# Selecting four features per row once for six products of a feature crossing, with grouped products and roundings

## The chip, the core and the metric

One NeuronCore of a Trainium2 chip runs the whole program. The metric is the device time of one execution in microseconds; lower is better. TensorE (PE) multiplies matrices into PSUM, VectorE (DVE) and ScalarE (ACT) do elementwise work and copies, GpSimd (POOL) starts the gathers from the embedding tables, SyncE (SP) starts the other transfers.

## What is computed

A recommender's forward pass for 512 samples with 39 categorical features. Each feature of a sample is looked up as a vector of 16 numbers; e has the shape 512 x 39 x 16. Two layers of a feature crossing follow, then a small dense tower:

```python
# _cin(e, [W0, W1]); m, n run over features, d over the 16 numbers
z  = einsum('bmd,bnd->bdmn', e, e)          # all 39 x 39 products per number
X1 = einsum('bdp,po->bod', z, W0)           # 1521 x 128
z  = einsum('bmd,bnd->bdmn', e, X1)
X2 = einsum('bdp,po->bod', z, W1)           # 39*128 x 128
h  = concat([sum_d(X1), sum_d(X2), dense_ctx])   # 512 x 272
h  = relu(h @ W_top1 + b1); h = relu(h @ W_top2 + b2); y = h @ W_top3
```

Everything is in float32, and the kernel keeps that precision on fast matmuls by splitting operands: a number is rounded to the fast format (high part), the remainder is kept (low part), and three products (high x high, high x low, low x high) stand for one.

## The kernel before

The batch is four tiles of 128 samples. A tile is cut into four chunks of 32 samples, and a chunk's 32 x 16 = 512 columns are the moving operand. So there are 16 chunks.

The first layer needs only the products of unordered pairs of features: 39 x 40 / 2 = 780. They are laid out as 7 groups of rows (PT = 7): six of 128 pairs, and the last one with the 12 pairs left over, each three times (REST_AT), for the three products of the split. A *step* s is one such group; 7 steps make a chunk, 28 a tile (SPT), and 112 (STEPS) the batch. The features of a tile, turned to have features on the partitions, are in `xs` as three bf16 parts. In a step, PE picks one factor of each pair with a 0/1 matrix (`select`, L904) into one of two PSUM banks (`b_bank`); the other factor, `xa`, is the same for all steps, since row p of every group has feature p % 39 as its first factor. It is copied out of PSUM once per chunk (`fill_a`, `take_a`, L882, L423). DVE multiplies (`multiply`, L716) into `z`, ACT rounds to `z_hi` (`round_z`, L529), DVE takes the remainder `z_lo` two steps later (`rest_z`, L730), and PE sums with the weights `w0_hi`, `w0_lo` five steps later (LAG; `layer1`, L919 to L927). In tile 0 two of the seven groups (DIRECT) skip the split: PE multiplies them in whole float32. `z_hi` and `z_lo` have seven slots (RING), one for each step in flight, so a step overwrites the slot of seven steps before, which PE has used two steps ago. `z` has four.

After the seven groups of a chunk ACT copies `xi` (L545), PE turns it (L934), ACT and DVE split it (L551, L737), and four times per chunk PE forms a block of g (L949 to L951) in the single bank `g_bank`, which ACT copies out (`take_g`, L537) before the next block may start. The x side for this is made by `turn_a` (L891), `take_xt`, `rest_xt` and transfers into `diag`. Layer 2 (L964) uses g a tile later, 39 matmuls for a tile, spread over 26 steps (12 for tile 2).

There is no scheduler: each engine runs one loop over s with the offsets written out, and executes its instructions strictly in the order of that loop, waiting on semaphores. The offsets within a chunk (steps modulo 7): `turn_a` at 1; `fill_a` of the next chunk at 4; g blocks at 3, 5, 0, 2; copy of xi at 4, its turn at 6. The order on ACT within a step is rounding, split copies, `take_g`, `take_xi`, `round_xit`, `take_xt`, `take_a`, `take_x`. The order on PE is selection, `turn_a`, `turn_x`, `turn_xi`, g block, layer 2, `fill_a`, layer 1.

The features come in two ways: small tables by one-hot products in the first 35 us, the others by 98 indirect DMAs which GpSimd starts one after another, with a filler memset between two of them. A tile's features are split into three bf16 parts in three pieces (`SPLIT_AT`: steps of the tile before; `keep_top` and `keep_next` on ACT, L475 and L481; `rest_hi` and `rest_mid` on DVE, L634 and L641), then turned on PE in two halves (`X_AT`, L860), each copied by ACT (`take_x`, L414), and then the first `xa` chunk of the tile is filled (`A_AT`).

## Time and profile before

| | |
|---|---|
| median of 3 runs | 263.35 us (263.24 to 263.35) |
| profiled execution | 262.94 us |
| its span, first to last instruction | 260.9 us |
| mean granted TensorE clock | 0.961 |
| busy: PE, DVE, ACT, POOL | 235.9, 196.1, 168.6, 128.8 us |

Busy time is the time with an instruction running on the engine. In a list of groups, `out<-in` names the tensors, then come shapes and counts, busy time, mean duration in ns, and the idle time right before such instructions with what ended it. In a timeline the first two numbers are start and duration in us; a square bracket gives idle time before the instruction and what released it. Durations of neighbours on one engine can overlap. The granted clock is the share of full speed (2.4 GHz) which TensorE was given.

### The profile page before, as it was taken

The page shows a single profiled execution, that of the slowest core. Times are in us where ns is not written, and L with a number is a line of the kernel's source. Part 1 is how long each engine was busy: PE and PEld are TensorE (multiplying, and loading weights), DVE is VectorE, ACT ScalarE, POOL GpSimd, SP SyncE. Part 2 cuts the span into 40 slices and gives each one's busy share as a digit, 9 for nine tenths or more (in the row PEclk, how much of TensorE's full clock was granted, in tenths as well). Part 3 has the DMA queues.
Part 4 walks back from the last instruction along what each step waited for, and adds up shares of the span by engine and source line. Part 5 has one row for each costly group of instructions (what it writes and reads, how often), then busy time and mean ns, then how long its engine had stood idle before and what let it go on. Part 6 is the DMA issues. An engine that isn't in the chain of part 4 may idle for free.

```text
span 260.9 us, 5243 instructions
## 1 busy us (share of the span) xinstructions
PE 235.9 (90%) x1848; PEld 182.4 (70%) x1848; DVE 196.1 (75%) x341; ACT 168.6 (65%) x324; POOL 128.8 (49%) x180
## 2 busy tenths in 40 slices
PE   4998856989799978939999999999999999999996
PEld 4997733555466754737777777777787888898795
DVE  1799969998879999556889999879989877624001
ACT  4997555675787886547759878686757655466203
POOL 4788888888888888878888882000000000000000
PEclk9999755899999999988999999999999999999999
DMA  5920001545026540200221111010110101010000
GB/s 160 233 45 10 9 5 13 112 83 129 8 27 147 122 96 7 28 8 9 45 33 20 24 11 28 5 25 7 21 16 12 25 1 25 4 25 0 3 0 0
DMA packets 30883, 10.30 MB, mean 39 GB/s; under 512 B 21018, under 2 KB 30138, under 8 KB 30858
## 3 DMA queue, kind: packets, MB, share of 16 engines
q1 hardware_dynamic: 27722, 9.17, 16.3%
q0 software_dynamic: 3136, 0.81, 3.5%
q8 instruction: 14, 0.23, 0.4%
q14 instruction: 11, 0.09, 0.1%
HBM read 7.34 MB, written 0.00 MB: 28 GB/s over the span
## 4 chain that ended last, share of the span: by engine, by line
PE 48%; POOL 26%; DVE 12%; issue 9%; ACT 3%; DMA 2%; DVEq 0%; ACTq 0%
POOL feat L355 21%; PE s_bank L964 11%; POOL pad L353 5%; PE b_bank L904 4%; PE l_bank L925 4%; PE l_bank L927 4%; PE l_bank L926 4%; DVE z L716 3%; DVE w_sb L660 3%; DVE z_lo L730 3%; PE g_bank L949 2%; PE g_bank L950 2%; PE g_bank L951 2%; PE xi_bank L934 1%; ACT g L448 1%
## 5 line engine op out<-in xcount | busy, mean ns | idle before, releaser
L355 POOL DMA_INDIRECT feat<-tbl,ids_sb x98 | 107.3, 1095 | 29.4 <-POOL pad L353 21.1
L716 DVE TENSOR_TENSOR z<-xa,b_bank 128x512 f32<-128x512 f32 (+1 forms) x112 | 76.1, 684 | 17.3 <-PE b_bank L904 13.8
L529 ACT ACTIVATE z_hi<-z 128x512 fp32r<-128x512 f32 (+1 forms) x104 | 65.6, 630 | 18.9 <-DVE z L716 17.5
L730 DVE TENSOR_TENSOR z_lo<-z,z_hi 128x512 fp32r<-128x512 f32 x88 | 60.3, 686 | 0.0
L904 PE MATMUL b_bank<-xs,sel 117*128 117x512 bf16 (+1 forms) x112 | 45.2, 406 | 8.7 <-DVE z L716 8.6
L964 PE MATMUL s_bank<-g,w_sb 128*128 128x128 f32 x312 | 46.3, 278 | 0.0
L964 PEld LDWEIGHTS s_bank<-g,w_sb 128*128 128x128 f32 x312 | 42.2, 192 | 1.3 <-issue 0.7
L925 PE MATMUL l_bank<-z_hi,w_hi 128*128 128x512 f32 x88 | 41.8, 474 | 0.0
L904 PEld LDWEIGHTS b_bank<-xs,sel 117*128 117x128 bf16 (+1 forms) x112 | 11.5, 103 | 38.3 <-DVE z L716 20.7
L537 ACT ACTIVATE g<-g_bank 128x320 f32<-128x320 f32 x64 | 27.7, 432 | 16.3 <-PE g_bank L951 16.0
L927 PE MATMUL l_bank<-z_hi,w_lo 128*128 128x512 f32 x88 | 35.1, 399 | 0.0
L926 PE MATMUL l_bank<-z_lo,w_hi 128*128 128x512 f32 x88 | 35.0, 398 | 0.0
L949 PE MATMUL g_bank<-diag,xit_hi 128*128 128x320 f32 x64 | 29.5, 462 | 3.2 <-ACT g L537 3.2
L353 POOL MEMSET pad<- 128x192 f32 x78 | 21.3, 273 | 0.1
L950 PE MATMUL g_bank<-diag,xit_hi 128*128 128x320 f32 x64 | 20.1, 313 | 0.0
L951 PE MATMUL g_bank<-diag,xit_lo 128*128 128x320 f32 x64 | 19.9, 310 | 0.0
L927 PEld LDWEIGHTS l_bank<-z_hi,w_lo 128*128 128x128 f32 x88 | 16.8, 191 | 3.8
L949 PEld LDWEIGHTS g_bank<-diag,xit_hi 128*128 128x128 f32 x64 | 12.6, 197 | 8.1 <-issue 5.9
L925 PEld LDWEIGHTS l_bank<-z_hi,w_hi 128*128 128x128 f32 x88 | 17.1, 194 | 1.3 <-issue 0.8
L926 PEld LDWEIGHTS l_bank<-z_lo,w_hi 128*128 128x128 f32 x88 | 17.1, 194 | 0.2
L545 ACT ACTIVATE xi<-l_bank 128x512 f32<-128x512 f32 x16 | 9.6, 597 | 9.0 <-PE l_bank L922 9.0
L560 ACT ACTIVATE g<-b_bank,bt_sb 128x384 f32<-128x384 f32 (+1 forms) x8 | 3.7, 473 | 15.8 <-PE b_bank L1005 11.0
(190 smaller groups left out, 368.2 us busy)
## 6 DMA issues: line engine op xcount, KB each, us to landing
diag<-xt SPq DMA_DIRECT2D x128, 20.0 KB
w_sb<-w SPq DMA_DIRECT2D x3, 832.0 KB
feat<-tbl,ids_sb POOLq DMA_INDIRECT x98, 2.4
wt_sb<-wt SPq DMA_DIRECT2D x2, 512.0 KB, 4.7
g<-small SPq DMA_DIRECT2D x1, 770.0 KB
g<-small SPq DMA_DIRECT2D x1, 448.0 KB
w0p<-w_pair SPq DMA_DIRECT2D x1, 448.0 KB
w0m<-w_mirror SPq DMA_DIRECT2D x1, 448.0 KB
```

The costliest lines, as they stand in the source:

```text
L353: nc.gpsimd.memset(pad[:], 0.0).then_inc(rested, 1)
L355: nc.gpsimd.indirect_dma_start(feat[:, bt % 2, n * D:(n + 1) * D], None, tables[order[n]], bass.IndirectOffsetOnAxis(ids_sb[:, bt, order[n ...
L529: nc.scalar.activation(z_hi[0:rows, s % RING, :], z[0:rows, at, :], ACT.Copy).then_inc(rounded, 1)
L537: nc.scalar.activation(g[:, bt % 2, :, block * SB:(block + 1) * SB], g_bank[:, 0:SB * GW].rearrange("p (b m) -> p m b", m=GW), ACT.Copy).t ...
L716: nc.vector.tensor_tensor(target, xa[0:rows, bt % 2, c * CB:(c + 1) * CB, :].rearrange("p b d -> p (b d)"), b_bank[s % B_RING][0:rows, :], ...
L730: nc.vector.tensor_sub(low[first:rows, s % RING, :], z[first:rows, SPLITS[s] % Z_RING, :], z_hi[first:rows, s % RING, :].bitcast(f32)).the ...
L904: nc.tensor.matmul(b_bank[s % B_RING][0:ROWS[t], :], sel[:, t, 0:ROWS[t]], columns(bt, c), start=True, stop=True).then_inc(selected, 1)
L925: nc.tensor.matmul(bank[:], w0_hi[:, t, :], z_hi[:, slot, :], start=t == 0, stop=False)
L926: nc.tensor.matmul(bank[:], w0_hi[:, t, :], z_lo[:, slot, :], start=False, stop=False)
L927: nc.tensor.matmul(bank[:], w0_lo[:, t, :], z_hi[:, slot, :], start=False, stop=False).then_inc(l1_used, 1)
L949: nc.tensor.matmul(o, y_hi, x_hi, start=True, stop=False)
L964: last = nc.tensor.matmul(s2_bank[:, 0:P], w1_sb[:, order[m], :], g[:, bt % 2, m, :], start=m == 0, stop=m == F - 1)
```

## The change

1. **Rows.** The pairs are laid out anew. Each row has four features (from the 130 lines of a block design on 40 points, of which one is no feature), and a row's six products of two of the four are the six full groups. All 741 mixed pairs and the 39 squares are covered, with the last ones in the rest group, now on all 128 rows.
2. **Selections.** Per chunk one x copy (`fill_a`) and four selections (before: one and seven). The first two are copied to SBUF by ACT (`take_factor`, new; DVE takes one of them in chunk 0), the other two are read from PSUM. The products are f0f1, f0f2; then f0 times the rest factor; then f3 times f0, f1, f2; then f1f2. `turn_a` reads factor 0.
3. **Groups.** Multiplication, rounding and remainder come as four instructions per chunk (of 2, 1, 3 and 1 groups of rows) in steps 0, 2, 3 and 6 of the chunk; the remainders in steps 2, 4, 6 and 8. The rest group is third instead of last. The slots of `z_hi` and `z_lo` are fixed by the group, so a rounding waits until PE has used all its slots for the chunk before.
4. **Whole products.** One per chunk of tile 0 instead of two.
5. **Offsets.** The splits of tiles 2 and 3 move from steps 8, 14, 19 and 9, 16, 21 of the tile before to 9, 16, 23; their turns from 21, 22 and 23, 24 to 25, 26; the x copy from 24 and 26 to 27. The first chunk of these tiles has its selections in its own steps 0, 0, 1, 2 instead of ahead of it.
6. **Small ones.** `w0_rest` is made by two multiplications with 0/1 columns instead of three copies, ahead of DVE's copy of the first features.

The diff, cut to its core:

```diff
-PT = -(-PAIRS // P)
-REST = PAIRS - (PT - 1) * P
-REST_AT = (0, F, 2 * F)
-REST_LO = 64
-REST_ROWS = 96
-ROWS = [P] * (PT - 1) + [REST_ROWS]
-assert REST <= F and REST_AT[1] >= 32 and REST_AT[1] + REST <= REST_LO <= REST_AT[2] and REST_AT[2] + REST <= REST_ROWS
+PT = 7
+FACTORS = 4
+PRODUCTS = ((0, 1), (0, 2), (3, 0), (3, 1), (3, 2), (1, 2))
+REST_T = PT - 1
+REST_LO = slice(64, 98)
+T_OF = (0, 1, REST_T, 2, 3, 4, 5)
+GROUPS = ((0, 2, 0, 0), (2, 1, REST_T, 2), (3, 3, 2, 3), (6, 1, 5, 2))
+GROUP_AT = {first: k for k, (first, count, slot, at) in enumerate(GROUPS)}
+REST_AT_STEP = {2: 0, 4: 1, 6: 2, 8: 3}
+GROUP_OF = [next(k for k, g in enumerate(GROUPS) if g[0] <= u < g[0] + g[1]) for u in range(PT)]
+NG = len(GROUPS)
+SELECTS = 4
...
-DIRECT = [[1, 4], [], [], []]
+DIRECT_CHUNKS = 4
 WHOLE = 2
-Z_LAG = 2
-Z_RING = Z_LAG + 2
-LEAD = 1
+Z_SLOTS = 6
...
-SPLIT_AT = [[], [8, 14, 19], [8, 14, 19], [9, 16, 21]]
-X_AT = [[], [21, 22], [21, 22], [23, 24]]
-A_AT = [0, 24, 24, 26]
+SPLIT_AT = [[], [8, 14, 19], [9, 16, 23], [9, 16, 23]]
+X_AT = [[], [21, 22], [25, 26], [25, 26]]
+A_AT = [0, 24, 27, 27]
+SELECT_AT = [-4, -2, -1, 0]
+TILE_SELECT_AT = [None, [-4, -2, -1, 0], [0, 0, 1, 2], [0, 0, 1, 2]]
...
             def take_a(i):
-                bt, c = divmod(i, CPT)
                 act.wait_ge(*after(turn_filled, "a", i, 0))
                 k = fill["a", i, 0][0]
-                nc.scalar.activation(xa[:, bt % 2, c * CB:(c + 1) * CB, :],
-                                     turn_banks[k][:].rearrange("p (b d) -> p b d", d=D),
-                                     ACT.Copy).then_inc(turn_taken[k], 1)
+                if i >= 2:
+                    act.wait_ge(product, NG * (i - 1))
+                nc.scalar.activation(factors[:, i % 2, 0, :], turn_banks[k][:], ACT.Copy).then_inc(turn_taken[k], 1)
+
+            def take_factor(i, k):
+
+                act.wait_ge(selected, SELECTS * i + k + 1)
+                if i >= 2:
+                    act.wait_ge(product, NG * (i - 1))
+                nc.scalar.activation(factors[:, i % 2, 1 + k, :], b_bank[k][:], ACT.Copy).then_inc(factor_taken, 1)
...
-            def round_z(s):
-                rows = ROWS[s % PT]
-                if direct(s):
+            def round_z(i, k):
+                if direct(i, k):
                     return
-                at = SPLITS[s] % Z_RING
-                act.wait_ge(product, s + 1)
-                if s >= RING:
-                    act.wait_ge(l1_used, s - RING + 1)
-                nc.scalar.activation(z_hi[0:rows, s % RING, :], z[0:rows, at, :], ACT.Copy).then_inc(rounded, 1)
+                first, count, slot, at = GROUPS[k]
+                act.wait_ge(product, NG * i + k + 1)
+                if i:
+                    act.wait_ge(l1_used, (i - 1) * PT + first + count)
+                nc.scalar.activation(z_hi[:, slot:slot + count, :], z[:, at:at + count, :],
+                                     ACT.Copy).then_inc(rounded, 1)
...
+                for i, q in SELECT_STEPS.get(s, []):
+                    if q < 2 and i:
+                        take_factor(i, q)
+                if s < STEPS and s % PT in GROUP_AT:
+                    round_z(s // PT, GROUP_AT[s % PT])
...
+            def z_free(i, k):
+
+                if (i, k) in SPLITS:
+                    dve.wait_ge(remainder, SPLITS[i, k] + 1)
+
+            def multiply(i, k):
...
+                if k == 0:
+                    for q in range(2):
+                        dve.wait_ge(*taken_factor(i, q))
+                    dve.wait_ge(*after(turn_taken, "a", i, 0))
+                    z_free(i - 1, 0)
+                    target = z[:, 0:2, :]
+                    one = factors[:, i % 2, 0, :].unsqueeze(1).broadcast_to([P, 2, CH])
+                    other = factors[:, i % 2, 1:3, :]
+                elif k == 1:
+                    dve.wait_ge(selected, SELECTS * i + 3)
+                    z_free(i - 1, 1)
+                    z_free(i - 1, 3)
+                    target, one, other = z[:, 2, :], factors[:, i % 2, 0, :], b_bank[0][:]
+                elif k == 2:
+                    dve.wait_ge(selected, SELECTS * i + 4)
+                    z_free(i - 1, 2)
+                    target = z[:, 3:6, :]
+                    one = factors[:, i % 2, :, :]
+                    other = b_bank[1][:].unsqueeze(1).broadcast_to([P, 3, CH])
                 else:
+                    if direct(i, k):
+                        if i == 0:
+                            dve.wait_ge(zeroed, 4)
+                        if i >= WHOLE:
+                            dve.wait_ge(l1_used, (i - WHOLE + 1) * PT)
+                        target = whole[i % WHOLE][:]
+                    else:
+                        z_free(i, 1)
+                        target = z[:, 2, :]
+                    one, other = factors[:, i % 2, 1, :], factors[:, i % 2, 2, :]
+                nc.vector.tensor_tensor(target, one, other, ALU.mult).then_inc(product, 1)
...
+            def rest_z(i, k):
+                if direct(i, k):
                     return
+                first, count, slot, at = GROUPS[k]
+                dve.wait_ge(rounded, SPLITS[i, k] + 1)
+                if i:
+                    dve.wait_ge(l1_used, (i - 1) * PT + first + count)
+                if k == 1:
+                    nc.vector.tensor_sub(z_hi[REST_LO, slot, :], z[REST_LO, at, :],
+                                         z_hi[REST_LO, slot, :].bitcast(f32)).then_inc(remainder, 1)
+                else:
+                    nc.vector.tensor_sub(z_lo[:, slot:slot + count, :], z[:, at:at + count, :],
+                                         z_hi[:, slot:slot + count, :].bitcast(f32)).then_inc(remainder, 1)
...
-            def select(s):
-
-                i, t = divmod(s, PT)
-                bt, c = divmod(i, CPT)
-                if s >= B_RING:
-                    pe.wait_ge(product, s - B_RING + 1)
-                if t == 0:
+            def select(i, q):
+
+                if q == 0:
                     features_there(i)
-                nc.tensor.matmul(b_bank[s % B_RING][0:ROWS[t], :], sel[:, t, 0:ROWS[t]], columns(bt, c),
+                if q < 2:
+                    if i:
+                        pe.wait_ge(product, NG * (i - 1) + 2 + q)
+                else:
+                    pe.wait_ge(*taken_factor(i, q - 2))
+                nc.tensor.matmul(b_bank[q % B_RING][:], sel[:, q, :], columns(*divmod(i, CPT)),
                                  start=True, stop=True).then_inc(selected, 1)
...
+                for i, q in SELECT_STEPS.get(s, []):
+                    select(i, q)
```

## Rows read from the trace of the kernel before

**Rows 1.** The page: the span, and each engine's busy time and share.

```profile
span 260.9 us, 5243 instructions
...
PE 235.9 (90%) x1848; PEld 182.4 (70%) x1848; DVE 196.1 (75%) x341; ACT 168.6 (65%) x324; POOL 128.8 (49%) x180
```

**Rows 2.** Busy us by stretch: PE, weight loads, DVE, ACT, POOL, granted clock, DMA.

```profile
66.00:108.00 42.00, 37.32 (x197) 25.59 (x198) 39.11 (x69) 32.17 (x67) 35.10 (x51) 1.00 0.32 66
115.00:120.00 5.00, 4.45 (x27) 3.68 (x28) 3.93 (x8) 3.63 (x8) 4.18 (x8) 0.66 0.06 8
165.00:208.00 43.00, 42.90 (x270) 33.68 (x270) 37.08 (x64) 29.20 (x58) 0.00 (x0) 1.00 0.10 16
```

**Rows 3.** The chain that ended last: start, us, what.

```profile
111.15 2.36 DMA feat<-tbl,ids_sb
...
119.35 0.37 PE turn_bank L891 x4
...
131.26 0.37 PE turn_bank L891 x4
...
177.85 0.37 PE turn_bank L891 x4
...
189.09 0.37 PE turn_bank L891 x4
...
200.54 0.37 PE turn_bank L891 x4
...
213.12 0.37 PE turn_bank L891 x4
```

**Rows 4.** Timeline at the gather of tile 2: start, us, instruction, idle before.

```profile
113.54 0.42 ACT L475 ACTIVATE parts<-feat 128x128 bf16<-128x128 bf16 x1 [4.48 <-DMA feat<-tbl,ids_sb]
...
114.48 0.39 PE L904 MATMUL b_bank<-xs,sel 117*128 117x512 bf16 x1 [3.67 <-DVE z L716]
```

**Rows 5.** Timeline of ACT in tile 2: start and duration in us.

```profile
168.64 1.02 ACT L414 ACTIVATE xs<-turn_bank 117x1024 bf16<-117x1024 bf16 x1
...
172.23 0.60 ACT L545 ACTIVATE xi<-l_bank 128x512 f32<-128x512 f32 x1
172.73 0.62 ACT L529 ACTIVATE z_hi<-z 128x512 fp32r<-128x512 f32 x1
```

**Rows 6.** Timeline of DVE: the first product, and two instructions back to back.

```profile
39.49 0.69 DVE L716 TENSOR_TENSOR z<-xa,b_bank 128x512 f32<-128x512 f32 x1
...
172.48 0.68 DVE L730 TENSOR_TENSOR z_lo<-z,z_hi 128x512 fp32r<-128x512 f32 x1
173.08 0.67 DVE L716 TENSOR_TENSOR z<-xa,b_bank 96x512 f32<-96x512 f32 x1
```

**Rows 7.** Groups by line: out<-in, shapes, busy us, mean ns.

```profile
L793 DVE TENSOR_TENSOR z_lo<-wt_sb,z_hi 128x1024 fp32r<-128x1024 f32 x1 | 1.2, 1227 | 0.4 <-ACT z_hi L591 0.4
...
L583 ACT ACTIVATE wt_hi<-wt_sb 128x1024 fp32r<-128x1024 f32 x1 | 1.1, 1062 | 0.0
```

**Rows 8.** Timeline of PE: transposes, a selection, the three products of layer 1.

```profile
167.12 0.66 PE L860 MATMUL turn_bank<-id,parts 128*117 128x128 bf16 x8
167.58 0.39 PE L949 MATMUL g_bank<-diag,xit_hi 128*128 128x320 f32 x1
...
171.35 0.39 PE L904 MATMUL b_bank<-xs,sel 117*128 117x512 bf16 x1
171.57 0.39 PE L964 MATMUL s_bank<-g,w_sb 128*128 128x128 f32 x2
...
181.79 0.48 PE L925 MATMUL l_bank<-z_hi,w_hi 128*128 128x512 f32 x1
...
182.58 0.39 PE L904 MATMUL b_bank<-xs,sel 117*128 117x512 bf16 x1
```

**Rows 9.** Timeline: a g_bank copy and the PE product behind it.

```profile
104.14 0.42 ACT L537 ACTIVATE g<-g_bank 128x320 f32<-128x320 f32 x1
...
104.70 0.39 PE L949 MATMUL g_bank<-diag,xit_hi 128*128 128x320 f32 x1 [0.69 <-ACT g L537]
```

270 lines of the change are left out of this document (151 added, 119 removed).

## Prediction

> **What bounds the kernel now.** I read the page first (spans and engines), then the busy time by stretch, then the chain of work that ended last, then the timeline around the places that the chain names. The page says that PE is busy for 90% of the span and DVE for 75% [rows 1]. That average hides two regimes. From 66 to 108 us DVE works 39.1 of 42 us and PE 37.3; from 165 to 208 us PE works 42.9 of 43 us and DVE 37.1 [rows 2]. Between them lies a hole. GpSimd's gathers run at an even pace, and the last one for tile 2 lands at 111.15 + 2.36 = 113.51 us [rows 3]. ScalarE starts on it at 113.54 us after 4.48 us of idleness, and TensorE resumes at 114.48 us after 3.67 us [rows 4]. The next 5 us run at a granted clock of 0.66, so partly at the lower level of 1.2 GHz [rows 2]. Behind that the transposes of the features (one per chunk) beat the time: 119.35, 131.26, 177.85, 189.09, 200.54, 213.12 us [rows 3], so a chunk costs 11.24 us, then 11.45 us, where PE is the bound, and 12.58 us where layer 2 of tile 2 is crowded in.
>
> **Prices.** Durations overlap a little, so I take start to start where an engine is full. ACT: a 512-column copy out of PSUM 0.50 us (172.23 to 172.73), though its result is there only after 0.60; I take the same tenth off the others, 0.52 for a rounding of 512, 0.92 for a copy of features, 0.33 for one of g [rows 5, 9]. DVE: 512 columns 0.60 us (172.48 to 173.08), duration 0.68 [rows 6]. The wide forms are not in the main loop, so I bound them: the 1024-column copy took 1.06 us and the 1024-column subtraction 1.23 us [rows 7]; against the 512 forms that is 0.83 and 1.06 ns a column. So 1536 columns are 1.47 us on ACT (1.38 start to start) and 1.77 us on DVE (1.67). Lower end for 1536: one and a half times the 1024 form without any fixed part, about 1.4 and 1.65; upper end: three of the 512 forms, 1.8 and 2.05. I take the straight line, as the 1024 rows lie on it. PE: a selection 0.22 us (171.35 to 171.57; 0.23 taken, with its weights), the three products of one layer-1 step 0.79 us (181.79 to 182.58), eight transposes of the next tile 0.46 us (167.12 to 167.58) [rows 8]. From the end of an ACT copy of g_bank to the PE product that waits for it: 104.14 + 0.42 to 104.70, 0.14 us [rows 9].
>
> **The change part by part.**
>
> *Selections.* Three of seven per chunk go: 3 x 0.23 = 0.69 us of PE, 5.5 us over the eight chunks of tiles 2 and 3. Where PE is full this would come straight off 11.24, to 10.55 us.
>
> *Products and remainders.* DVE keeps the columns and loses three multiplications and three subtractions per chunk as instructions: 14 x 0.60 = 8.4 us becomes two of each 512 form, one 1024 (1.14) and one 1536 (1.67) each, 4 x 0.60 + 2 x 1.14 + 2 x 1.67 = 8.0 us. So DVE gains only 0.4 us a chunk. Tile 0 loses one of its two whole products per chunk: one more split there, 0.6 us less saved, nothing on PE's path, since PE has spare time there.
>
> *ACT.* Rounding: 7 x 0.52 = 3.6 us becomes 0.95 + 1.38 + 2 x 0.52 = 3.4 us; two copies of selected factors are new, 1.0 us. ACT stays under 9 us a chunk, so it is no bound by its sum. But it is one queue, and this is where the change bites.
>
> *Ring A, on ACT and DVE.* The three-product multiplication (group 2, step 3 of a chunk) releases, one behind the other on ACT: the 1536 rounding 1.38, the g_bank copy 0.33, xi 0.50, the next chunk's first factor 0.50, its second factor 0.59. Only then can DVE start the next chunk: 3.4 us with hops. DVE then does 1.14 (two products), the xi remainder 0.60 after a short wait of 0.3, a remainder 0.60, a product 0.60, the 1024 remainder 1.14, 0.22, and the three products 1.77: 6.4 us. The ring is 9.8 us, 9.2 in tile 0, where one remainder is missing. A feature split adds 0.3 to 0.5 on DVE and 0.3 to 0.75 on ACT. It binds until the gather.
>
> *Ring B, on PE and ACT.* The 1536 rounding overwrites slots which PE uses until the last product of the same step 3 (before, the slot had been free for two steps). Behind it on ACT stands the g_bank copy, and for that waits PE's g product of step 5. From PE's last product of step 3: 0.2 to ACT, 1.38, 0.43, 0.14 = 2.15 us. PE has the work of step 4 and a selection meanwhile, about 1.55 us. So it stalls 0.6 us in each chunk: 10.55 + 0.6 = about 11.1 us, and of the 0.69 saved 0.1 is left. A split adds its second copy (0.35 to 0.75) to the stall.
>
> *Splits four steps later.* The third split of tile 2 moves from step 19 to 23 of tile 1, transposes from 21 and 22 to 25 and 26, the next tile's x copy from 24 to 27. This lets four steps go ahead of the gather. Starting at 39.9 us (the first product of the kernel before is at 39.49 [rows 6]; the two weight instructions for w0_rest go into DVE's wait before it), ring A gives 8.0, 9.3, 9.4, 9.7, 9.8, 10.9 and 10.4 us for chunks 0 to 6 (less in chunk 0, where nothing is behind it; splits and the copies of the features are in the others). Chunk 7 starts at 107.4 us and DVE is at the split at 112.0. The gather lands at 113.5: a stall of 1.5 us in place of the 4 to 5. Then ACT 0.33, the g copy 0.33, and PE's step 3 (0.42 + 1.11): the rounding of chunk 7 starts at 116.2 us.
>
> *What the move costs at a tile's start.* From that rounding (0): 1.38, second split copy until 1.80, PE's transposes only at 1.90 (PE has waited since step 3), first features copy 2.55 to 3.45, g copy 4.85, second features copy until 5.87, PE's turn of xi at 5.95, its step 6 until 7.5, x selection and two factor selections until 8.2, three ACT copies until 9.5, and DVE begins the new tile at 9.6 where ring A would allow 3.4. Then DVE 6.1 more; PE also waits for the g copy behind the first rounding, and both end near 15.7. So a tile's first chunk costs 15.6 us from rounding to rounding against 11.1. In the kernel before, four chunks with a change of tile (131.26 to 177.85) took 46.6 us, 1.4 to 1.7 over four plain ones. The change costs some 3 us more at each of two tiles.
>
> *The Trainium skill against it.* In the kernel before PE met a single late g copy here and there, with 0.69 us of idle in the row [rows 9]. The Trainium skill, "Perfetto Trace Analysis", section "Optimizing Scalar/DVE Operations", says that larger operations help a saturated engine, but where Scalar or Vector are not saturated and cause bubbles on others, breaking them up may be right. By that rule the ACT half of the grouping is a loss; with the 1536 rounding as three pieces ring B would have no stall, and my sum would be 3 to 4 us lower.
>
> **The sum.** From rounding to rounding, chunk 7 to 15: 15.6 + 11.1 + 11.2 + 11.45 + 15.6 + 11.1 + 10.9 + 13.5 = 100.5 us (third and fourth with a split and without layer 2 in two steps; the last two as in the kernel before, where layer 2 pauses for two steps and is then crowded in). 116.2 + 100.5 = 216.7. In the kernel before the same point lies some 6.2 us after the transpose at 213.12, at 219.3. That is 2.6 us gained. In chunk 15 five selections still ahead go (1.1) and a stall of 0.6 comes: 0.5 more. PE idles twice around 112 to 118 us, and the clock may fall as it did at 115 (5 us at 0.66, worth 1.7 us): I take 0.6 of it; ends 0 and 1.7. The profiled execution took 262.94 us (span 260.9 and 2.0 around it, 0.4 under the median): 262.94 - 2.6 - 0.5 + 0.6 = 260.4 us.
>
> **Rivals.**
> - *Work alone counts*: neither ring shows, a tile's start costs what it does now. Rounding of chunk 8 at 116.2 + 10.55 + 1.55 = 128.3 us, its transpose about 123.3 against 131.26, and seven chunks less 0.69 each: 12.8 us at chunk 15, 1.1 behind it: 249 us. For it: PE is the bound by rows; against it: the order on ACT is strict. Chance 0.15.
> - *Slower: ring A holds full latencies.* If its instructions don't overlap (0.68, 0.60 and 0.14 for each hand-over in place of 0.60 and 0.50), the ACT part is 3.9 and the DVE part 7.1: 11.0 us a chunk. Chunk 7 then starts at 115.2, its rounding is at 122.6, 6.4 later than above; a tile's first chunk costs 17.2 and the plain ones up to 11.5: 272 us. It decides from about 10.4 us a chunk in tile 1: there the gather is missed by the 2.5 us that I expect to gain. For it: DVE is busy for 39.1 of 42 us between 66 and 108 us [rows 2], so small waits of some 0.7 us a chunk come in even where it is the bound. Chance 0.27.
> - *The two moves cancel* (gather stall gone, tile starts dearer, rings even): 262.4 to 263.4. Chance 0.08.
>
> My own case, 256.5 to 262.4, has 0.50. The predicted time is its sum. The range that should hold 8 in 10 is 253 to 270, from between mine and the first rival to near the second. A measurement tells 0.2% (0.5 us) from no change. Faster: 0.50 + 0.15 = 0.65; within: 0.08; slower: 0.27.
>
> **What would show it.** Right: PE waits at the first g_bank product for ACT once per chunk, about 0.6 us; ACT's 1536 copy near 1.47 us, DVE's near 1.77; feature transposes 11.1 us apart in tile 3's plain chunks; the first chunk of tiles 2 and 3 some 4.5 us longer than its neighbours; a gather stall of 1 to 2 us at 113.5. Wrong: feature transposes 10.6 us apart (first rival); tile 1's chunks over 10.4 us apart and no stall at the gather (second); wide forms far off the straight line.

## The result, and the profile after

The changed kernel takes 270.4 us (median of 6 runs, 269.97 to 273.29) against 263.35 (6 runs, 262.86 to 264.29): 1.028 times as long, with a 95% interval of 1.023 to 1.033. The prediction was 260.4 us, faster. Its profiled execution took 270.33 us, with a span of 268.3.

The page of the changed kernel (busy us, share of the span, instructions), as [rows 1] for before:

```profile
span 268.3 us, 4963 instructions
PE 228.4 (85%) x1804; PEld 179.1 (67%) x1804; DVE 194.0 (72%) x249; ACT 177.0 (66%) x311; POOL 131.6 (49%) x180
```

TensorE does 7.5 us less, VectorE 2.1 less, ScalarE 8.4 more, and the span is 7.4 us longer. So the question is where TensorE waits. Busy us by stretch in the changed kernel (stretch, its length, then PE, weight loads, DVE, ACT and POOL, granted clock, DMA); the first three answer to [rows 2]:

```profile
66.00:108.00 42.00, 35.74 (x181) 24.87 (x182) 36.40 (x43) 33.51 (x63) 35.05 (x51) 0.96 0.29 64
115.00:120.00 5.00, 5.00 (x35) 4.41 (x34) 4.87 (x8) 2.96 (x6) 4.18 (x7) 1.00 0.09 8
165.00:208.00 43.00, 38.16 (x239) 30.01 (x239) 32.63 (x39) 29.63 (x53) 0.00 (x0) 1.00 0.08 13
...
120.00:124.00 4.00, 1.96 (x18) 1.48 (x17) 3.17 (x5) 2.11 (x3) 3.19 (x7) 1.00 0.22 37
124.00:128.00 4.00, 3.14 (x26) 2.56 (x25) 0.30 (x1) 3.27 (x5) 3.46 (x5) 1.00 0.27 49
128.00:132.00 4.00, 4.00 (x27) 2.95 (x26) 1.02 (x1) 2.17 (x4) 3.18 (x7) 1.00 0.12 23
```

The hole at the gather is gone: PE works all of 115 to 120 us, at the full clock. But from 165 to 208 us, where PE had been busy for 42.90 of 43 us, it is now busy for 38.16; and a new hole has opened at the start of tile 2, 120 to 128 us, where PE misses 2.9 us, and DVE works 1.3 of the 8 us from 124 to 132.

One time per chunk is enough to lay the two kernels side by side: the start of `turn_a` (L891 before, L950 after), called the x turn here. It is read from the timeline of PE in every run. "Chunks 0 to 7" is the time from the first x turn to the eighth, "chunks 7 to 15" from there to the sixteenth and last. Two of the profiles below, `e2_g_first` and `r2_after_again`, are of executions some 2.5% and 1.2% longer than those kernels' medians.

| us | first x turn | chunks 0 to 7 | chunks 7 to 15 | last x turn to the end |
|---|---|---|---|---|
| before | 40.8 | 78.5 | 93.8 | 47.9 |
| after | 40.3 | 75.9 | 103.1 | 49.0 |

From chunk to chunk: before 8.3, 8.8, 12.5, 9.8, 9.3, 10.7, 19.3, 11.9, 11.2, 12.0, 10.6, 12.8, 11.2, 11.5, 12.6; after 9.7, 9.2, 14.4, 10.0, 9.4, 10.9, 12.2, 14.8, 12.6, 13.5, 10.8, 14.8, 12.6, 11.6, 12.3. So 7.1 us are gained at the gather (19.3 to 12.2) and 4.5 of them had been lost before it; then 9.3 are lost in eight chunks and 1.1 in the tail.

What ended the idle time, in the changed kernel: engine and line that waited, what for, us, times, longest:

```profile
ACT z_hi L562 <- PE l_bank L986: 17.5, 17, 3.0
DVE z L776 <- ACT factors L458: 14.3, 5, 6.7
PE g_bank L1008 <- ACT g L571: 13.9, 17, 1.7
```

The third line is ring B of the prediction. In the view of all that touches `g_bank`, the line "sat idle until" shows it at its clearest, because it takes in the weight loads too. The changed kernel:

```profile
  ACT g L571: 29.6, 31
```

The kernel before:

```profile
  ACT g L537: 3.8, 7
```

The first chunk of tile 3 (chunk 12) in the changed kernel, ACT and PE (start, us, instruction, idle before it and its releaser):

```profile
183.98 1.06 ACT L562 ACTIVATE z_hi<-z 128x1024 fp32r<-128x1024 f32 x1 [1.35 <-DVE z L776]
184.94 0.42 ACT L571 ACTIVATE g<-g_bank 128x320 f32<-128x320 f32 x1
...
185.41 0.41 PE L1008 MATMUL g_bank<-diag,xit_hi 128*128 128x320 f32 x1 [0.89 <-ACT g L571]
...
189.03 1.49 ACT L562 ACTIVATE z_hi<-z 128x1536 fp32r<-128x1536 f32 x1 [0.91 <-DVE z L776]
190.42 0.42 ACT L571 ACTIVATE g<-g_bank 128x320 f32<-128x320 f32 x1
...
190.89 0.41 PE L1008 MATMUL g_bank<-diag,xit_hi 128*128 128x320 f32 x1 [0.45 <-ACT g L571]
```

The g copy stands behind a wide rounding at two places of a chunk. The second was in the prediction. The first, behind the 1024-column rounding of group 0, was not, and in this chunk it is the dearer one. Not every chunk has both waits: from chunk 6 on PE's g product waits twice in chunks 6, 8, 9 and 12, once in 10 and 13 (0.61 us there), and not in 7, 11 and 14.

The start of tile 2 in the changed kernel, from the rounding of chunk 7:

```profile
121.02 1.48 ACT L562 ACTIVATE z_hi<-z 128x1536 fp32r<-128x1536 f32 x1 [2.12 <-PE l_bank L986]
122.41 0.41 ACT L514 ACTIVATE parts<-rest 128x128 bf16<-128x128 bf16 x1
...
122.96 0.63 PE L920 MATMUL turn_bank<-id,parts 128*117 128x128 bf16 x8 [2.04 <-ACT parts L514]
...
124.59 0.60 ACT L579 ACTIVATE xi<-l_bank 128x512 f32<-128x512 f32 x1 [1.45 <-PE l_bank L986]
125.08 1.02 ACT L441 ACTIVATE xs<-turn_bank 117x1024 bf16<-117x1024 bf16 x1
...
126.30 1.05 ACT L441 ACTIVATE xs<-xi_bank 117x1024 bf16<-117x1024 bf16 x1
127.49 0.63 PE L993 MATMUL xi_bank<-id,xi 128*128 128x128 f32 x4 [0.86 <-ACT xs L441]
128.88 0.39 PE L942 MATMUL turn_bank<-xs,sel 117*128 117x512 bf16 x1
```

Everything hangs on one string: second split copy, transposes, features copies, x selection, factor copies; DVE's next product comes at 130.98 us, 9.96 after the rounding.

### The profile page after: what moved, and what is told of

The parts are those of the page before. It is cut to its first block, busy times and chain, and to the rows that moved or that the text cites. A ratio compares the mean times of both kernels' runs of the same rounds, so it can differ in the third digit from the quotient of the medians.

```text
span 268.3 us, 4963 instructions
## 1 busy us (share of the span) xinstructions
PE 228.4 (85%) x1804; PEld 179.1 (67%) x1804; DVE 194.0 (72%) x249; ACT 177.0 (66%) x311; POOL 131.6 (49%) x180
## 4 chain that ended last, share of the span: by engine, by line
PE 48%; DVE 21%; issue 14%; ACT 14%; DMA 1%; DVEq 0%; ACTq 0%
PE s_bank L1023 10%; DVE z L776 7%; PE l_bank L984 5%; DVE w_sb L697 4%; PE l_bank L986 4%; PE l_bank L985 4%; PE g_bank L1008 4%; DVE z_lo L789 3%; ACT g L571 3%; PE xi_bank L993 2%; PE b_bank L964 2%; PE g_bank L1010 2%; PE g_bank L1009 2%; ACT parts L514 2%; ACT xs L441 1%
## 5 line engine op out<-in xcount | busy, mean ns | idle before, releaser
L382 POOL DMA_INDIRECT feat<-tbl,ids_sb x98 | 110.1, 1124 | 29.4 <-POOL pad L380 21.1
L562 ACT ACTIVATE z_hi<-z 128x512 fp32r<-128x512 f32 (+2 forms) x60 | 58.7, 978 | 37.8 <-DVE z L776 19.9
L789 DVE TENSOR_TENSOR z_lo<-z,z_hi 128x1024 fp32r<-128x1024 f32 (+2 forms) x44 | 56.0, 1274 | 9.6 <-ACT z_hi L562 8.9
L984 PE MATMUL l_bank<-z_hi,w_hi 128*128 128x512 f32 x92 | 44.9, 488 | 0.0
L776 DVE TENSOR_TENSOR z<-factors 128x1024 f32<-128x1024 f32 (+1 forms) x32 | 30.7, 958 | 15.4 <-ACT factors L458 14.3
L776 DVE TENSOR_TENSOR z<-factors,b_bank 128x512 f32<-128x512 f32 (+1 forms) x32 | 38.9, 1214 | 1.1
L1008 PE MATMUL g_bank<-diag,xit_hi 128*128 128x320 f32 x64 | 25.6, 399 | 15.1 <-ACT g L571 13.9
L964 PE MATMUL b_bank<-xs,sel 117*128 117x512 bf16 x64 | 26.4, 423 | 5.2 <-DVE z L776 4.8
L1008 PEld LDWEIGHTS g_bank<-diag,xit_hi 128*128 128x128 f32 x64 | 12.2, 190 | 23.4 <-ACT g L571 15.6
L964 PEld LDWEIGHTS b_bank<-xs,sel 117*128 117x128 bf16 x64 | 6.5, 101 | 24.0 <-issue 13.6
L458 ACT ACTIVATE factors<-b_bank 128x512 f32<-128x512 f32 x31 | 18.4, 600 | 3.7 <-PE b_bank L964 3.6
L1009 PE MATMUL g_bank<-diag,xit_hi 128*128 128x320 f32 x64 | 19.8, 309 | 0.0
```

The source lines that it names most:

```text
L382: nc.gpsimd.indirect_dma_start(feat[:, bt % 2, n * D:(n + 1) * D], None, tables[order[n]], bass.IndirectOffsetOnAxis(ids_sb[:, bt, order[n ...
L562: nc.scalar.activation(z_hi[:, slot:slot + count, :], z[:, at:at + count, :], ACT.Copy).then_inc(rounded, 1)
L776: nc.vector.tensor_tensor(target, one, other, ALU.mult).then_inc(product, 1)
L789: nc.vector.tensor_sub(z_lo[:, slot:slot + count, :], z[:, at:at + count, :], z_hi[:, slot:slot + count, :].bitcast(f32)).then_inc(remaind ...
L964: nc.tensor.matmul(b_bank[q % B_RING][:], sel[:, q, :], columns(*divmod(i, CPT)), start=True, stop=True).then_inc(selected, 1)
L984: nc.tensor.matmul(bank[:], w0_hi[:, t, :], z_hi[:, t, :], start=u == 0, stop=False)
```

## The experiments

Two things are to be told apart: ring B (a g copy behind a wide rounding) and the late splits (the string at a tile's start). Rivals are a DVE or ACT that is slow by itself in the new grouping, and, for the gain that did not come, the gather.

One thing has to be known to read the numbers. On most of the chips used, the loop started at 50 to 59 us and not at 40, with the kernel before too; the prologue had stretched. There the gather of tile 2 is early enough to stop nobody, while the kernel before takes 272 to 283 us. The total times that the first expectations name were meant for a start at 40 us, so they can't be held against these runs. So a ratio is given beside the kernel before on the same chip, and mechanisms are compared by the stretches between x turns. For most kernels there is one trace, and a stretch moves by 1 to 2 us between traces of one kernel on two chips (chunks 0 to 7 of after: 75.9 and 74.3).

### Each kernel again

The kernel before:

> The kernel before once more, unchanged, for its trace beside the others on the same chip: in the first four experiments the loop started at 53 to 59 us in place of 40, by the chip and not by the kernel. Both theories: from the first x turn to the end 220 us where the loop starts at 40 us, 214 to 216 where it starts so late that no engine waits for the gather of tile 2.

The changed kernel:

> The changed kernel once more, unchanged. Both theories: 228 us from the first x turn to the end, wherever the loop starts, since it meets no gather late; chunks 7 and 11 take 14.8 us from x turn to x turn.

| us | first x turn | chunks 0 to 7 | chunks 7 to 15 | tail |
|---|---|---|---|---|
| before, again | 53.0 | 76.4 | 95.1 | 47.9 |
| after, again | 54.8 | 74.3 | 104.7 | 49.1 |

The ratio is 1.024 (1.016 to 1.032). Behind the gather the difference is 9.6 us, near that of the first pair (9.3). It is not exact: the tile starts of after took 15.3 and 15.9 us here, 14.8 in the first.

### The old splits

```diff
-SPLIT_AT = [[], [8, 14, 19], [9, 16, 23], [9, 16, 23]]
-X_AT = [[], [21, 22], [25, 26], [25, 26]]
-A_AT = [0, 24, 27, 27]
-TILE_SELECT_AT = [None, [-4, -2, -1, 0], [0, 0, 1, 2], [0, 0, 1, 2]]
+SPLIT_AT = [[], [8, 14, 19], [8, 14, 19], [8, 14, 19]]
+X_AT = [[], [21, 22], [21, 22], [21, 22]]
+A_AT = [0, 24, 24, 24]
+TILE_SELECT_AT = [None, [-4, -2, -1, 0], [-4, -2, -1, 0], [-4, -2, -1, 0]]
```

> The changed kernel with the splits of tiles 2 and 3 where tile 1 has them (8, 14, 19; turns at 21 and 22; x copy at 24; selections ahead of the tile). Theory Q (the time went into ACT's queue, at the tile starts above all: 16.3 us from rounding to rounding at chunks 8 and 12 against 11.4): tile starts fall to about 13 us, 7 us less in all, and about 2 us of waiting for the gather at 113.5 us comes back: 264 to 267 us. Rival M (the later splits are what keeps the kernel from losing more at the gather): 271 to 275 us.

Chunks 7 to 15 took 95.8 us, 7.3 less than in after. The two tile starts went from 14.8 + 12.6 to 12.1 + 11.2 us and from 14.8 + 12.6 to 12.1 + 11.2 again (a tile's first x turn is late too, so two intervals belong to each); the chunks between gave back 1.1. From the first x turn to the end it is 220.4 us against 228.0. So the late splits cost 7 to 8 us, and ring B stays: the tail is 49.1. The ratio, 1.032 (1.015 to 1.049), says little here, as the kernel before took 266 to 282 us on that chip; from the first x turn to the end it takes 219.4 and 220.2 us in its two traces.

### The move alone, in the kernel before

The constants of the first three lines of that diff, set the other way in the kernel before.

> The kernel before with the later splits alone (9, 16, 23; turns at 25 and 26; x copy at 27). Theory Q: the 4 to 5 us of waiting at the gather of tile 2 go, each tile start costs 1 to 2 us more, since here only one copy stands between the x selection and the first product: 259 to 263 us. Rival M2 (the move by itself is what made the change slower): 266 us or more.

Chunk 6 to 7 went from 14.8 us (`r1_before_again`) to 12.7. That isn't the wait for the gather: in the trace of `r1_before_again` no engine waits for the gather of tile 2. What has left this interval are the third split and the turns behind it, where PE was idle for 1.5 us just before the x turn. The tile starts went from 11.9 to 13.8 and from 12.8 to 13.8, and chunks 7 to 15 together from 95.1 to 98.1. So the move by itself costs 3.0 behind the gather and brings 2.1 there, read from one trace each, on two chips. What it brings where the gather binds was not run. Together with the selections of the new kernel, which also come late, it costs 7.3. The four runs took 271.7 to 279.5 us; there is no ratio for them.

### The g copy ahead of the rounding

ACT's queue puts `take_g` before `round_z` in each step:

```diff
+                for r, at in enumerate(G_AT):
+                    if (i := chunk_at(s, at)) is not None:
+                        take_g(SUBS * i + r)
                 if s < STEPS and s % PT in GROUP_AT:
                     round_z(s // PT, GROUP_AT[s % PT])
```

> The changed kernel with ACT's copy of g_bank put ahead of the roundings within each step, nothing else. Theory Q, ring B (PE's g product of step 5 waits for the g copy behind the 1536-column rounding): the waits of PE for that copy, 13.9 us, mostly go, and 3 to 5 us of the time: 265 to 268 us. Rival W (the wide instructions and the two factor copies cost by their work, order is no matter): within 1 us of 270.4.

Chunks 0 to 7 took 73.5 us (75.9, and 74.3 on the second chip), 7 to 15 took 97.8 (103.1), the tail 47.2 (49.0). The ratio to the kernel before on that chip is 1.014 (1.005 to 1.022): still a little slower, with the late splits still in. The view of all that touches `g_bank`, the line for ACT's copy:

```profile
  ACT g L571: 1.3, 3
```

29.6 us of idle on PE and its loads went to 1.3. The three chunks of tile 3 up to the last x turn (12 to 15) tell it best. Busy us, columns as above. The kernel before:

```profile
177.82:213.09 35.27, 35.27 (x217) 27.74 (x216) 30.72 (x52) 22.99 (x46) 0.00 (x0) 1.00 0.09 15
```

The changed kernel:

```profile
182.69:219.25 36.56, 34.47 (x208) 27.22 (x207) 32.34 (x38) 25.34 (x44) 0.00 (x0) 1.00 0.09 14
```

With the g copy ahead:

```profile
196.37:230.21 33.84, 33.82 (x208) 27.26 (x208) 31.70 (x37) 23.97 (x44) 0.00 (x0) 1.00 0.10 16
```

Before, PE is full and takes 35.27 us. After, it has nine instructions less and is idle for 2.1 us: 36.56. With the g copy ahead it is full again. The kernel with both edits (below) has 10.5, 10.8 and 11.9 us for these chunks, against 11.2, 11.5 and 12.6 before: 0.7 us each, the three selections as forecast. The kernel before with the same order and schedule (`e13_before_schedule`, below) has 11.2, 11.5 and 12.6 too, so the 0.7 is not the schedule's. Ring B took back nearly all of it: with the early schedule and the g copy behind (`e7_both_turns_early`, below) the three take 11.2, 11.6 and 12.3, 1.9 us more than with the copy ahead. The rest of the 36.56 us is the late tile start, which reaches into the first of the three (12.7 in place of 11.2).

### Three roundings in place of the wide one

ACT's 1536-column rounding as three of 512, each with its own wait for its slot; DVE is left as it is.

> The changed kernel with the 1536-column rounding issued as three of 512, each waiting for its own slot. Theory Q: ACT has the same columns and about 0.16 us more to do, but after PE's last product of step 3 only 0.5 us of rounding stand before the g copy in place of 1.4: 0.6 us less a chunk where PE is the bound, 266 to 269 us. Rival G (grouping saves fixed costs and helps): 271 to 273 us.

Chunks 0 to 7 took 74.0 us, 7 to 15 100.8, the tail 48.1: 5.1 us less than after from the first x turn on, 3.2 of them from the eighth; the other 1.9 are hardly more than the 1.6 by which after's own two traces differ. The four runs took 277.6 to 284.1 us, with the loop starting at 53.5; there is no ratio for them. PE's wait for the copy went from 13.9 us (17 times) to:

```profile
PE g_bank L1015 <- ACT g L578: 9.5, 11, 1.6
```

The prediction had said that such pieces leave no stall, worth 3 to 4 us. The worth was about right and the reason half so. In chunks 13 and 14 no wait is left, and they take 10.8 and 11.9 us, as with the copy ahead. In chunks 8, 9 and 12 the waits remain, the one at the 1024-column rounding unchanged (0.89 us in chunk 12). The Trainium skill, "Perfetto Trace Analysis", section "Optimizing Scalar/DVE Operations", says that breaking up instructions may help where Scalar or Vector are not saturated but cause bubbles on other engines; the trace agrees (ACT is busy for 66%), and here changing the order did more than breaking up.

### The same order in the kernel before

> The kernel before with ACT's g copy ahead of the rounding, nothing else: the control for ring B. There the rounding is 512 columns wide and its slot has been free for two steps, so ring B doesn't exist: within 1 us of the 219 to 220 us from the first x turn to the end. Rival (the order of the g copy is worth something in any kernel, and the changed one only shows it): 215 or less.

Ratio 0.998 (0.995 to 1.002); chunks 7 to 15 took 94.4 us against 93.8. In the kernel before the order of the two copies is worth nothing. So ring B belongs to the new grouping and not to the queue as such. The grouping has two sides, the width of a rounding and the wait for slots that PE frees late; the control doesn't tell them apart.

### Is ACT's chain what binds tiles 0 and 1?

The copy of `xi` one step later takes 0.5 us out of the chain that the prediction calls ring A.

> The changed kernel with ACT's copy of xi one step later, behind the next chunk's second factor copy, nothing else. Ring A (three products, rounding, g, xi, x and factor copies on ACT, next products): it loses the 0.48 us of that copy in each chunk of tiles 0 and 1, so the seven chunks between the first and the eighth x turn take 72.5 to 74 us in place of 75.9, the rest about the same: 225 to 226 us from the first x turn to the end. Rival D (in tiles 0 and 1 the work of DVE is the bound): 75.5 or more for the seven chunks.

Chunks 0 to 7 took 75.5 us against 75.9 (74.3 on the second chip), the rest as in after (103.6 and 49.1), ratio 1.010 (1.004 to 1.017) to the kernel before on that chip. A ring through that copy alone would have given 0.5 us in each of seven chunks, 3.5 us. The edit isn't clean, though: DVE's wait for the rounding of `xit`, which comes behind the same copy, rose from 4.3 to 8.4 us in all, and from 0.3 to 2.4 in these seven chunks. So the run leans against ring A and doesn't exclude it. The timeline of DVE in chunk 1 of after says more:

```profile
48.79 1.22 DVE L776 TENSOR_TENSOR z<-factors 128x1024 f32<-128x1024 f32 x1
...
51.14 1.22 DVE L789 TENSOR_TENSOR z_lo<-z,z_hi 128x1024 fp32r<-128x1024 f32 x1
52.72 0.32 DVE L803 TENSOR_TENSOR xt<-turn_bank,xt 128x156 fp32r<-128x156 f32 x1 [0.36 <-ACT xt L464]
...
58.73 1.22 DVE L776 TENSOR_TENSOR z<-factors 128x1024 f32<-128x1024 f32 x1
```

DVE is full: 9.94 us from first product to first product, with one wait of 0.36 us and small gaps where a wide remainder follows its rounding. The forecast for this chunk was 9.3. Between x turns DVE is idle for 0.2, 0.6, 1.9, 2.8, 0.8, 0.5 and 0.7 us in chunks 0 to 6: DVE is nearly full in all but chunk 2, where it waits for a gather (1.49 us), and chunk 3, where tile 1 starts.

### An earlier tile start

Splits at 9, 16, 21, turns at 23 and 24, the x copy at 25, selections of the new tile from three steps ahead:

```diff
-SPLIT_AT = [[], [8, 14, 19], [9, 16, 23], [9, 16, 23]]
-X_AT = [[], [21, 22], [25, 26], [25, 26]]
-A_AT = [0, 24, 27, 27]
-TILE_SELECT_AT = [None, [-4, -2, -1, 0], [0, 0, 1, 2], [0, 0, 1, 2]]
+SPLIT_AT = [[], [8, 14, 19], [9, 16, 21], [9, 16, 21]]
+X_AT = [[], [21, 22], [23, 24], [23, 24]]
+A_AT = [0, 24, 25, 25]
+TILE_SELECT_AT = [None, [-4, -2, -1, 0], [-3, -2, -1, 0], [-3, -2, -1, 0]]
```

> The changed kernel with the third split of tiles 2 and 3 at step 21, turns at 23 and 24, x copy at 25, and the selections of a tile's first chunk ahead of it (-3, -2, -1, 0) as in any other chunk. Theory Q: a tile start costs by its order (two factor copies only after the x copy, all in the new tile), so each of chunks 7 and 11 falls from 14.8 to about 12.3 us and chunks 8 and 12 from 12.6 to 11.5: 6 to 8 us less than the changed kernel, of which up to 2 are given back at the gather if the loop starts at 40 us. Rival X (the tile start costs by the work of the feature turn and its two copies): 0 to 2 us less.

Chunks 7 to 15 took 103.0 us: no gain. The first chunk of tile 2 took 16.9 instead of 14.8. The timeline of ACT and PE there:

```profile
130.88 1.48 ACT L562 ACTIVATE z_hi<-z 128x1536 fp32r<-128x1536 f32 x1 [1.70 <-PE l_bank L986]
132.27 0.42 ACT L571 ACTIVATE g<-g_bank 128x320 f32<-128x320 f32 x1
132.59 1.01 ACT L441 ACTIVATE xs<-xi_bank 117x1024 bf16<-117x1024 bf16 x1
...
133.70 0.59 PE L964 MATMUL b_bank<-xs,sel 117*128 117x512 bf16 x1 [2.92 <-issue]
```

The second features copy has got behind the wide rounding, the first selection of the new tile waits for it, and PE, which is in order too, waits with it for 2.92 us. So I gave both turns the same step, 23, ahead of the rounding:

> As the experiment before with split 21, x copy 25 and early selections, but both halves of the next tile's features turned at step 23, so that ACT's two copies of them stand ahead of the 1536-column rounding of step 24 and not around it. Theory F (a tile start costs because ACT's second copy of features waits behind that rounding, and TensorE's next selection behind the copy: 2.9 us of idle and 3 us at a clock of 0.57): chunk 7 falls from 16.9 to 13 us and chunk 11 from 15.6 to 13 us; from the first x turn to the end 220 to 222 us (226 there, 228 in the changed kernel). Rival X (the work of the turn itself costs): 225 or more.

Now 96.7 us for chunks 7 to 15, 6.4 less than in after, with tile starts of 13.1 us. The same two schedules with the g copy ahead as well:

> That, and ACT's g copy ahead of the roundings. Theory Q: both gains add up, as they are at different places (the second was 9.5 us from the first x turn to the end: 218.5 in place of 228.0): 211 to 214 us from the first x turn to the end, and 254 to 258 us in all where the loop starts at 40 us, faster than both kernels. Rival W: no less than the better of the two alone.

> That with ACT's g copy ahead of the roundings. Theory F with ring B: 211 to 214 us from the first x turn to the end, against 218.5 with both as they stood; 6 us or more under the kernel before on the same chip. Rival: the sum of both is not reached, since ring A holds the time: 216 or more.

And the g copy ahead with the old splits:

> The changed kernel with the earlier splits (8, 14, 19, selections ahead of the tile) and the g copy ahead of the roundings. The two were worth 7.6 and 9.5 us from the first x turn to the end where the loop starts so late that the gather is there. Theory Q: they are at different places and add up to 15 or so: 211 to 214 us. Rival: they take the same waits away: 217 to 219.

| us | chunks 0 to 7 | chunks 7 to 15 | tail | ratio to before, same chip |
|---|---|---|---|---|
| after | 75.9 | 103.1 | 49.0 | 1.028 (1.023 to 1.033) |
| e5, splits 21, turns 23 and 24 | 74.2 | 103.0 | 49.1 | 1.001 (0.996 to 1.007) |
| e6, the same and g first | 71.9 | 99.4 | 47.2 | 0.977 (0.965 to 0.990) |
| e7, splits 21, turns 23 and 23 | 75.9 | 96.7 | 49.1 | 0.987 (0.977 to 0.996) |
| e8, the same and g first | 73.4 | 93.4 | 47.2 | 0.958 (0.948 to 0.967) |
| e10, old splits and g first | 74.9 | 94.2 | 47.2 | 0.975 (0.967 to 0.983) |

The two causes don't simply add, as the expectations of `e6_both` and `e10_old_splits_g_first` had it (211 to 214 us from the first x turn to the end; 218.5 and 216.3 came, and 214.0 in `e8_combined`): the g copy is worth 5.3 us behind the gather on the late schedule, 3.6 and 3.3 on the earlier ones, 1.6 on the old one, and 1.8 or 1.9 in the tail on each. The early schedule is worth 6.4 without it and, from `e2_g_first`, 4.4 with it. Both together bring 9.7 us from the eighth x turn to the last, where after had lost 9.3.

### Back where the loop starts at 40 us

The combined kernel, with tile 1 on the same schedule as the others; and the kernel before with the g copy ahead and the new schedule of tiles 2 and 3 (both turns at 23). Both ran on a chip where the loop starts at 40 to 41 us.

> The best version so far (g copy first; both turns of tiles 2 and 3 at step 23) with the same schedule for tile 1, whose third split, turns and x copy were left at 19, 21, 22 and 24. Theory E (of the 5 us that the first seven chunks took beyond the forecast, most went at the third split of tile 1, where DVE, ACT and PE meet its gather and PE then runs at a clock of 0.66): the seven chunks take 71 to 72 us in place of 73.4. Rival (they went into small waits in all chunks): 73 or more.

> The kernel before with the g copy first and the third split, both turns and the x copy of tiles 2 and 3 at 21, 23 and 25: the schedule of the best version without its selections and grouping. Theory S (the saved selections are real work: 0.69 us of PE in each chunk of tiles 2 and 3): 4 to 6 us more than the best version's 214.0 from the first x turn to the end, 218 to 220. Rival (the best version is fast by its schedule alone): 213 to 216.

The first gave a ratio of 1.001 (0.998 to 1.004), the second 0.996 (0.993 to 0.999), the fastest of all there by a hair: here selections and grouping are worth nothing. For what the first was meant to test, the start of tile 1, it says little: chunks 0 to 7 took 72.5 us, and 73.8 when it was run again (`e16_all_tiles_again`), against 73.4 in `e8_combined`. The chunks of the first: 9.5, 9.5, 9.5, 13.1, 8.6, 10.6, 11.6, **19.2**, 10.5, 11.6, 10.0, **18.5**, 10.5, 10.8, 11.9. The same schedule had tile starts of 14.0 and 13.9 us in `e8_combined`. The timeline of ACT at the gather and of PE behind it:

```profile
116.11 0.42 ACT L508 ACTIVATE parts<-feat 128x128 bf16<-128x128 bf16 x1 [2.46 <-DMA feat<-tbl,ids_sb]
...
119.32 1.11 PE L920 MATMUL turn_bank<-id,parts 128*117 128x128 bf16 x8 [4.93 <-DVE xt L803]
```

Three stretches of the same kernel, columns as above, with the clock:

```profile
112.00:116.00 4.00, 2.40 (x16) 1.63 (x14) 0.73 (x2) 1.39 (x3) 3.19 (x6) 1.00 0.08 6
116.00:120.00 4.00, 0.68 (x6) 0.68 (x7) 3.89 (x7) 0.94 (x3) 3.45 (x6) 0.70 0.04 4
120.00:124.00 4.00, 4.00 (x23) 3.71 (x22) 1.68 (x3) 1.77 (x4) 3.19 (x6) 0.50 0.11 11
```

The gather binds again, as in [rows 4], and behind it TensorE was granted 0.50 (1.2 GHz) for 4 us after 4.93 us of idleness. From the split of tile 2 to the end it is 146.8 us here, 147.4 in the kernel before, 145.3 in `e13_before_schedule`. So where the loop starts at 40 us, all that lies ahead of the gather is worth nothing. But the gather is also later: the last one of tile 2 is issued at 113.8 us, against 111.2 before and 112.8 in `e13_before_schedule`, whose remainders are narrow.

The gather of tile 3 binds as well. ACT waits for it, and PE behind it:

```profile
166.29 0.42 ACT L508 ACTIVATE parts<-feat 128x128 bf16<-128x128 bf16 x1 [1.22 <-DMA feat<-tbl,ids_sb]
...
169.48 1.11 PE L920 MATMUL turn_bank<-id,parts 128*117 128x128 bf16 x8 [3.67 <-DVE xt L803]
```

Its last gather is issued at 163.7 us, in `e13_before_schedule` at 159.0, where nobody waits for it and the same chunk took 13.1 us in place of 18.5. So what the plain chunks of the new kernel gain is more than spent there.

### Why the gathers are later

In the timeline of `e11_all_tiles`, GpSimd's gathers take 0.95 us each at their shortest, with exceptions such as these two; above each, what DVE does:

```profile
98.17 1.75 DVE L789 TENSOR_TENSOR z_lo<-z,z_hi 128x1536 fp32r<-128x1536 f32 x1
...
98.30 2.45 POOL L382 DMA_INDIRECT feat<-tbl,ids_sb  x1 [0.27 <-POOL pad L380]
...
150.42 1.75 DVE L789 TENSOR_TENSOR z_lo<-z,z_hi 128x1536 fp32r<-128x1536 f32 x1
...
151.15 1.85 POOL L382 DMA_INDIRECT feat<-tbl,ids_sb  x1 [0.27 <-POOL pad L380]
```

The remainder ends at 99.92 and 152.17, the gather at 100.75 and 153.00: 0.83 us later both times. Of 12 gathers there that begin in a remainder of 1536 columns, 11 end 0.82 to 0.83 us after it; their mean is 1.66 us, that of the other 86 1.09. The 13 that begin in a product of 1536 columns, which is as long but has one operand in PSUM, took 0.95 us each. The kernel before has the same thing on a smaller scale: of the 15 gathers from 41 us on that begin in a 512-column remainder, 14 end 0.82 to 0.83 us after it, at 0.99 to 1.39 us. Three runs test it on one chip: the kernel again; DVE's remainder of group 2 as three of 512; the one of group 0 as two besides.

> The kernel of the run before with all tiles' splits at 9, 16, 21, both turns in step 23 and the g copy ahead of the rounding, once more, as the base for the next two on the same chip. If the loop starts near 40 us: some 264.3 us, a ratio to the kernel before of 0.998 to 1.004, the last gather of tile 2 started near 113.8 us and gathers of 1.16 us on average. If it starts past 50 us: a ratio near 0.96, as the gather is then early enough.

> The same kernel, but DVE's remainder of group 2 comes as three instructions of 512 columns in place of one of 1536. Theory: a gather that GpSimd begins while DVE runs that remainder ends only 0.82 to 0.83 us after the remainder's end (12 gathers of the kernel with all tiles moved, mean 1.66 us against 1.09 us of the others), so the wide remainder makes the last gather of tile 2 start 2.6 us later than in the kernel before (113.8 against 111.2 us), and the gather sets the time where the loop starts near 40 us. It expects there: no gather over 1.9 us in the main loop, the first 69 gathers 1.5 to 2.5 us shorter in sum (79.4 before the edit, 76.7 in the kernel before), the split of tile 2 begun by 114.5 in place of 116.1 us, 1.5 to 2.5 us less in all: 262 to 263 us, a ratio of 0.992 to 0.995. Rival: the gathers wait no less, since three pieces back to back keep GpSimd out as long as one; then the same time as before the edit or 0.5 us more, as DVE has 0.13 us more work in each chunk. Second rival: the gathers get shorter but the time stays, since what follows the landing has to wait for something else.

> Besides, the remainder of group 0 comes as two instructions of 512 columns in place of one of 1024. The theory expects a little more of the same, 0.2 to 0.7 us less than with the group of three alone in pieces, gathers at 1.09 to 1.11 us on average as in the kernel before (1.095), and no gather but those behind a 1024-column product over 1.5 us in the loop. The rival expects no gain, or a loss of up to 0.6 us where DVE is full ahead of the gather.

The gathers of tile 3, in the groups by line. The kernel before:

```profile
L355 POOL DMA_INDIRECT feat<-tbl,ids_sb x29 | 30.6, 1057 | 7.8 <-POOL pad L353 7.8
```

All tiles moved, `e11_all_tiles`:

```profile
L382 POOL DMA_INDIRECT feat<-tbl,ids_sb x29 | 34.2, 1178 | 7.9 <-POOL pad L380 7.9
```

The remainder of three in pieces, `e14_pieces_of_three`:

```profile
L382 POOL DMA_INDIRECT feat<-tbl,ids_sb x29 | 31.2, 1077 | 7.9 <-issue 5.7 <-POOL pad L380 2.2
```

In pieces they take 31.2 us, with both in pieces 31.1, in the base on the same chip 33.8. So the wide remainder lengthens them. The sums alone would be thin, at one trace each: the kernel before has 32.0 us in `r1_before_again`, and the changed kernel, wide remainders and all, 31.6. It is the ends of the single gathers that show the cause. For tile 2's 29 gathers the sums are less even: 32.0 before, 34.6 and 31.9 in the two runs of the base, 33.1 and 32.5 in pieces; it is a matter of which gathers fall in a remainder. What it is worth in time stays open: the chip of these three started its loop at 51 to 53 us, where no gather binds, and the ratios are 0.967 (0.960 to 0.975), 0.965 (0.958 to 0.971) and 0.970 (0.962 to 0.977), alike.

## Why the prediction was wrong, point by point

The profiled execution was 9.9 us over the sum (270.33 against 260.4). The rounding of chunk 7 starts at 121.0 us, not 116.2: 4.8 us. From there to the rounding of chunk 15 it takes 104.2 us, not 100.5: 3.7. The rest has 1.4 more, although the 0.6 us allowed for the clock were not needed: from 108 to 132 us it was 1.00.

- *Prices.* Right. The wide forms lie on the straight line: by form, 1485 and 1058 ns on ACT for 1536 and 1024 columns (1.47 and 1.06 forecast; the line itself gives 1.49, so the 1.47 was a slip), 1762 and 1745 ns on DVE for the remainder and the product (1.77).
- *Selections.* Right, 0.7 us a chunk, but only visible once ring B is gone.
- *Ring A.* This step failed, by 4.8 us. The working had a ring through ACT set the pace at 9.2 to 9.8 us a chunk; the runs show DVE full instead. The first products of chunks 0 and 6 are at 39.8 and 101.9 us, 62.1 apart where the working gave 57.1. From one to the next it is 9.0, 9.9, 11.0, 11.9, 9.4 and 10.9 us; forecast were 8.0, 9.3, 9.4, 9.7, 9.8 and 10.9. So the loss lies in the first four. DVE has little idle time in chunks 0 and 1, so small waits of some 0.6 us a chunk, which I had left to the second rival, come on top. The third split of tile 1 waits for its own gather: DVE is idle for 1.49 us at 67.03. The kernel before had that wait too (1.37 us at 65.78), and the working left it out; new is that PE's clock was 0.66 from 66 to 71 us, where it was 1.00 before. And tile 1's start has a string like that of tiles 2 and 3 (11.9 us, 2.2 over the forecast; PE waits 1.22 us for the features copy), for which the working had next to nothing. Behind that, the terms listed from the landing of the gather to the rounding of chunk 7 add up to 115.7 us and not to 116.2.
- *Ring B.* Right mechanism, and the size came out near, in part by luck. I had 0.6 us once per chunk, 4.8 in eight; the copy ahead brings 5.3 us in these eight, and 0.7, 0.8 and 0.4 in the three chunks of tile 3 on the early schedule. But the waits are not where I had them: they lie at two places, of up to 1.3 us in these chunks, and I had looked at the 1536-column rounding alone and not walked the g copy of step 0 behind the 1024-column one. In the tail the size was wrong: I had counted 0.6 us behind chunk 15, and it is 1.8 (49.0 against 47.2).
- *The end.* Besides that, I had counted five selections of chunk 15 as still ahead at the point where the sum ends (1.1 us). In the kernel before two are left there, at 219.19 and 220.33 us, some 0.5 us. With 1.2 us of ring B that is 1.8 of the 2.0 us that remain when the unused clock term is taken out.
- *Tile start.* Right in kind, and short: 16.3 us twice, not 15.6. The failed step is the first features copy, which I had at 2.55 us after the rounding and which came at 4.06. The copy of xi stands ahead of it in ACT's queue (the order that stands in the text), and xi waits for the layer-1 products of PE, which themselves had waited for the split. What I forecast as some 3 us at each of two tiles is 3.7 at each (7.3 in two, by `e1_old_splits`).
- *Chunk 9.* 12.5 us against 11.1: the context's copies and remainders (`ctx_whole`) lie in this chunk. They were in the kernel before too (12.0 between its x turns, 142.4 and 154.4), so this was a term left out.
- *The gather.* Wrong. I expected 1.5 us of stall; there is none, since the split is only at 117.4 us. The loop arrives behind the gather, as the second rival had said it would.
- *The rivals.* The second came out: it had the rounding of chunk 7 at 122.6 us (121.0), 17.2 for a tile's first chunk (16.3), up to 11.5 for plain ones (11.4) and 272 us (270.4). That it came so near is luck. It had ACT's chain at full latencies make 11.0 us of a chunk, and the first products of chunks 1 and 4 are followed by the next after 9.9 and 9.4 us; nor does `e9_xi_later` speak for that chain. The waits that it had spread over all chunks lay mostly at tile 1's gather and at the tile starts.

The pattern behind the misses: most parts were in the text, and each was sized at its first place only. Some five of the ten us (2.2 at tile 1's start, 1.3 at the two later ones, 1.2 in the tail) are waits in in-order queues that a walk through one whole chunk and one whole tile change for each engine would have shown.
